# A decoder of two layers on one core: the last layer's start moves into cross attention's last group, and TensorE multiplies for nobody in two waits

## The reference, cut to what matters

```python
x = LN(x + test_time_training(x))                 # a linear model, one SGD step per token
x = LN(x + cross_attention_0(x, ctx, mask))       # one head, width 256, bias 512 x 1601
x = LN(x + mixture_of_experts(x))                 # 8 experts, top 2, hidden 1024
x = LN(x + causal_self_attention(x))              # 16 heads of 16
x = LN(x + cross_attention_1(x, ctx))             # 16 heads of 16, rotary, out @ Wo.T + bo
h = (x - mean) * rsqrt(var) * gamma + beta        # layer norm inside the last block
x = LN(x + 0.5 * (silu(h @ W1 + b1) @ W2 + b2))   # W1, W2 dequantised, hidden 1024
```

## Time and profile before

| | |
|---|---|
| median of 3 runs | 2063.3 us |
| profiled execution | 2063.18 us, its span 2061.1 us |
| TensorE busy | 1811.4 us (88%), mean clock 0.936 |
| VectorE busy | 1428.5 us (69%) |
| ScalarE busy | 1063.8 us (52%) |
| GpSimd busy | 710.5 us (34%) |

### The profile page before, as it was taken

The page is one execution under the profiler, slowest core; times in us unless marked ns, Lnnn a source line. Parts: engine busy times, 40 slices in busy tenths (PEclk is TensorE's granted clock), DMA queues, the critical chain, the costliest instruction groups (busy, mean ns, idle before and its releaser), DMA issues. The chain is left out here.

```text
span 2061.1 us, 32786 instructions
## 1 busy us (share of the span) xinstructions
PE 1811.4 (88%) x12562; PEld 1031.0 (50%) x12562; DVE 1428.5 (69%) x2391; ACT 1063.8 (52%) x1706; POOL 710.5 (34%) x786
## 2 busy tenths in 40 slices
PE   8888888893999999947999989869999999998687
PEld 4677655672888888833333365512222222221455
DVE  1432368774677777767778558889999999991644
ACT  1111144450656555523666723318888888787242
POOL 0574286501344444423233014321541212100543
PEclk9999999995999999977899999959999999998789
DMA  5014087756466666534111037611311101000101
GB/s 183 19 62 135 35 296 249 257 205 251 180 258 263 259 249 239 184 115 131 25 32 34 9 132 212 198 37 58 95 47 24 34 17 34 17 17 1 51 1 41
DMA packets 107743, 241.62 MB, mean 117 GB/s; under 512 B 28362, under 2 KB 79086, under 8 KB 103600
## 3 DMA queue, kind: packets, MB, share of 16 engines
q1 hardware_dynamic: 80484, 199.43, 27.5%
q0 software_dynamic: 24992, 38.00, 6.6%
q10 hardware_dynamic: 2112, 2.10, 0.3%
HBM read 182.09 MB, written 56.79 MB: 116 GB/s over the span
## 5 line engine op out<-in xcount | busy, mean ns | idle before, releaser
L1772 DVE TENSOR_REDUCE Eh_maxima<-Eh_max 128x2 f32<-128x802 f32 x512 | 474.7, 987 | 22.9 <-PE Eh_max L1657 16.0
L1760 ACT ACTIVATE Eh_probs<-Eh_pair 128x1024 f32<-128x1024 f32 (+1 forms) x288 | 287.8, 999 | 117.0 <-PE Eh_pair L1696 117.0
L1152 PE MATMUL C_y<-C_x_high,C_W 128*128 128x256 f16 x1472 | 250.2, 274 | 1.5 <-DVE C_x_low L1389 1.5
L1657 PE MATMUL Eh_max<-Eh_KS,Eh_QS 49*128 49x401 f16 x1024 | 198.4, 358 | 51.9 <-DVE Eh_maxima L1772 41.7
L1719 PE MATMUL Eh_av_ps<-Eh_probs,E_V 128*17 128x512 f32 (+1 forms) x1664 | 226.0, 616 | 0.0
L1152 PE MATMUL C_y<-C_x_low,C_W 128*128 128x256 f16 x736 | 201.5, 274 | 0.0
L1772 DVE TENSOR_REDUCE Dh_maxima<-Dh_max 128x2 f32<-128x1024 f32 x128 | 152.1, 1221 | 46.7 <-PE Dh_max L1665 42.7
L1760 ACT ACTIVATE Eh_probs<-Eh_single 128x512 f32<-128x512 f32 x272 | 161.5, 594 | 21.3 <-PE Eh_single L1696 21.2
L1657 PEld LDWEIGHTS Eh_max<-Eh_KS,Eh_QS 49*128 49x128 f16 x1024 | 50.5, 94 | 240.8 <-DVE Eh_maxima L1772 201.3
L1500 POOL DMA_DIRECT2D Eh_KS<-E_kd x64 | 37.2, 582 | 356.5 <-PE Eh_pair L1696 350.7
L1152 PEld LDWEIGHTS C_y<-C_x_high,C_W 128*128 128x128 f16 x1472 | 144.6, 98 | 18.9 <-issue 1.9
(11 more groups left out here) (367 smaller groups left out, 3702.2 us busy)
## 6 DMA issues: line engine op xcount, KB each, us to landing
C_W<-w_split SPq DMA_DIRECT2D x23, 3072.0 KB, 11.1
w_split<-B_w_parts SPq DMA_DIRECT2D x24, 768.0 KB, 4.6
B_places<-in_w_experts_dram SPq DMA_DIRECT2D x18, 768.0 KB, 6.0
Eh_KS<-E_kd POOLq DMA_DIRECT2D x64, 150.1 KB, 3.3
C_tail<-in_expert_tail_dram SPq DMA_DIRECT2D x23, 384.0 KB, 8.0
A_QT<-in_w_experts_dram SPq DMA_DIRECT2D x8, 768.0 KB, 5.2
w_split<-A_QT SPq DMA_DIRECT2D x8, 768.0 KB, 6.8
early_ctxT<-in_ctxT_dram SPq DMA_DIRECT2D x6, 800.5 KB, 5.8
```

The source lines that it names most:

```text
L1152: last = mm(y_ps[n % Y_BANKS][:, i, :], W[:, u, a, at_w:at_w + P], x[:, s % 2, k, :], start=(q == 0), stop=(q == len(parts) - 1))
L1657: last = self.nc.tensor.matmul(bank[:, a, 0:self.cw], self.QS[r, slot, p, qt * P:(qt + 1) * P], self.KS[r, slot, p, k0:k0 + self.cw], star ...
L1760: self.nc.scalar.activation(dst, src, ACT.Exp, scale=1.0 / SCORE).then_inc(self.exp_done, 1)
L1772: self.nc.vector.tensor_reduce(self.maxima[:, g % 2, :, p * TPB + qt, c], self.max_ps[n % 2][:, :, 0:self.cw], AX_X, ALU.max).then_inc(sel ...
```

## The change

Nothing of what is computed changes. In parts:

1. `spin` is new: n float32 products of the identity with 512 columns, whose result nobody reads. Eight stand in TensorE's list before the first `turn` of the expert layer, thirteen, behind the wait for the weights, before the first `turn` of self attention.
2. In self attention's first stage VectorE normalises batch 0 before it begins to mix batch 1, and SP issues the loads of constants behind all loads of rows.
3. VectorE no longer waits for `all_stored` in `Heads`; to make that safe the small tiles of the maxima are placed with the keys and queries. Both `Heads` blocks leave out GpSimd's drain at the end.
4. A class `LastStart` holds what the last block begins with. Its 15 items (`START_ITEMS`) go into the last group of cross attention, the first behind its third S and then one behind every second S; all are shift, `attended` and `project` of batches 0 to 2, and the two half turns of batch 0's normalised tokens. They use the two banks of the maxima. VectorE does all copies, sums and norms there, GpSimd the bias additions, the inverse deviations and the low part of batch 0. The token of group 14 waits until the banks are free. SP loads Wo, bo, bv, gamma and beta before the first rows of maxima.
5. No barrier for clearing semaphores stands between cross attention and `phase_last`; that phase begins with turning batch 1. Batch 3's attention result is turned after four widenings of batch 0, projected in step 1 of batch 1; the turns of batches 2 and 3 come in step 5 of batches 1 and 2. W1's parts stay in SBUF (the weights' order is swapped, W2 is the one stored and loaded).

```diff
+def spin(nc, bank, ident, x, n):
+    for _ in range(n):
+        nc.tensor.matmul(bank, ident, x, start=True, stop=True)
@@ phase_moe, tensor
+            spin(nc, y_ps[0][:].rearrange("p a s -> p (a s)"), ident[:], XT[:, 0, 0:S], 8)
             turn(0)
@@ phase_self, sync
-                places.load_consts(sp)
                 for b in range(1, B):
...
+                places.load_consts(sp)
@@ phase_self, tensor
+                pe.wait_ge(carried.w_loaded, 32)
+                spin(nc, turn_ps[0][:], ident[:], w[:, 0, 0:S], 13)
                 turn(0)
-                pe.wait_ge(carried.w_loaded, 32)
@@ phase_self, vector
                 norm.statistics(dve, 0, sum_ready)
+                norm.normalize(dve, 0)
                 mix(1, 0)
-                norm.normalize(dve, 0)
                 rest_x(0)
@@ Heads.walk, last step of the walk
+            between = iter(range(len(START_ITEMS)) if self.start is not None and step == GROUPS - 1 else ())
+            scores = 0
             for kind in self.order:
+                if kind == "T":
+                    for i in between:
+                        yield "X", i
...
                 elif kind in "SB":
                     yield "S", s
-                    s += 1
+                    s, scores = s + 1, scores + 1
+                    if scores >= START_AFTER and (scores - START_AFTER) % 2 == 0:
+                        for i in between:
+                            yield "X", i
+                            break
@@ Heads.tensor
+            if kind == "X":
+                if k == 0:
+                    pe.wait_ge(self.read, n)
+                self.start.tensor(pe, START_ITEMS[k])
             if kind == "T":
+                if k == GROUPS - 2 and self.start is not None:
+                    self.start.banks_free(pe)
@@ Heads.vector
-        self.places.all_stored(dve)
...
+            if kind == "X":
+                self.start.vector(dve, START_ITEMS[k])
@@ run_heads
-    with nc.Block() as block:
+    with nc.Block(no_gpsimd_drain=True) as block:
...
+            if heads.start is not None:
+                heads.places.all_stored(sp)
+                heads.start.sync(sp)
@@ new
+START_ITEMS = (("shift",), ("attended", 0, 0), ("attended", 0, 1), ("attended", 1, 0), ("project", 0), ("attended", 1, 1), ("project", 1),
+               ("attended", 2, 0), ("project", 2), ("attended", 2, 1), ("project", 3), ("project", 4), ("project", 5), ("turn", 0), ("turn", 1))
+START_AFTER = 3
+class LastStart:
+    def vector(self, dve, item):
...
+        if kind == "project":
+            j = at[0]
+            after.add_pair(dve, j)
+            if j == 1:
+                after.norm.statistics(dve, 0, after.sum_ready, per=2)
+            if j == 2:
+                self.again(dve, 0)
+            if j == 3:
+                after.norm.statistics(dve, 1, after.sum_ready, per=2)
+            if j == 4:
+                self.normed_again(dve, 0)
+            if j == 5:
+                self.again(dve, 1)
+                after.norm.statistics(dve, 2, after.sum_ready, per=2)
+        if kind == "turn":
+            h = at[0]
+            dve.wait_ge(self.turned, h + 1)
+            v.tensor_scalar(self.HT[:, 0, h, :], after.turn_ps[h], self.gamma[:, h:h + 1], self.beta[:, h:h + 1], ALU.mult, ALU.add).then_inc(self.copied, 1)
+            if h == KD - 1:
+                dve.wait_ge(self.copied, KD)
+                v.tensor_copy(self.HT_parts[:, 0, 0], self.HT[:, 0]).then_inc(self.ht_high, 1)
+                self.normed_again(dve, 1)
+    def pool(self, pool):
...
+        for c in range(B - 1):
+            after.base(pool, c)
+        after.norm.inverse_deviation(pool, 0)
+        norm_in.inverse_deviation(pool, 0)
+        after.norm.inverse_deviation(pool, 1)
+        after.base(pool, B - 1)
+        norm_in.inverse_deviation(pool, 1)
+        after.norm.inverse_deviation(pool, 2)
+        self.low(pool, 0)
@@ phase_last, tensor (all of the old order up to the loop is gone)
             turn(1)
+            for j in range(NF // 2):
+                widen(0, j)
+            pe.wait_ge(copied, 2 * KD)
+            after.attended(pe, B - 1)
             for j in range(NF // 2, NF):
                 widen(0, j)
+            pe.wait_ge(w_loaded, 16)
             for c in range(1, B):
                 for j in range(NF):
                     widen(c, j)
                     narrow(c - 1, j // 2, range(NF // 2) if j % 2 == 0 else range(NF // 2, NF))
+                    if (c, j) == (1, 1):
+                        after.project(pe, B - 1)
+                    if (c, j) == (1, 5):
+                        turn(2)
+                    if (c, j) == (2, 5):
+                        turn(3)
@@ phase_last, scalar
+            act.wait_ge(small_loaded, 32)
             turn(1)
+            for n in range(B * NF):
                 step(n)
+                if n == NF // 2 - 1:
+                    copy_turned(nc, act, XT, turn_ps, B - 1, after.turned, after.copied)
+                if n == NF + 5:
+                    turn(2)
+                if n == 2 * NF + 5:
+                    turn(3)
@@ phase_last, gpsimd
+            norm_out.setup(pool)
+            start.low(pool, 1)
+            low(0)
             norm_in.inverse_deviation(pool, 2)
+            for n in range(1, B * NF):
+                low(n)
+                if n == NF + 1:
+                    after.norm.inverse_deviation(pool, 3)
+                if n == NF + 4:
+                    norm_in.inverse_deviation(pool, 3)
+                if n in (NF + 6, 2 * NF + 6):
+                    start.low(pool, n // NF + 1)
+                if n in (2 * NF + 1, 3 * NF + 1):
+                    norm_out.inverse_deviation(pool, n // NF - 2)
@@ phase_last, vector
+            dve.wait_ge(small_loaded, 32)
             v.tensor_scalar(b2[:], b2[:], 0.5, None, ALU.mult).then_inc(half_b2, 1)
+            step(0)
+            start.again(dve, 2)
+            step(1)
+            step(2)
             dve.wait_ge(half_b2, 1)
+            base(0)
+            for j in range(3, NF):
+                step(j)
             for c in range(1, B):
                 for j in range(NF):
                     step(c * NF + j)
+                    if (c, j) == (1, 0):
+                        start.normed_again(dve, 2)
+                    if (c, j) == (1, 1):
+                        after.add(dve, 3)
+                        after.norm.statistics(dve, 3, after.sum_ready, per=2)
...
+                    if (c, j) == (1, 4):
+                        start.again(dve, 3)
+                    if (c, j) == (2, 0):
+                        start.normed_again(dve, 3)
```

More of the change, by code:

```diff
@@ L1505, with __init__ @@
 class Heads:
-    def __init__(self, ctx, nc, name, n_keys, places, V, ATT, idents, tri, ahead, behind, order):
-        self.nc, self.n_keys, self.causal = nc, n_keys, places.causal
+    def __init__(self, ctx, nc, name, n_keys, places, V, ATT, idents, tri, ahead, behind, order, start=None):
+        self.nc, self.n_keys, self.causal, self.start = nc, n_keys, places.causal, start
         self.places, self.KS, self.QS, self.slots, self.R = places, places.KS, places.QS, places.slots, places.R
@@ L1520, in __init__ @@
         self.L = len(self.tiles)
-        self.chunks = (n_keys + S - 1) // S
+        self.chunks = places.chunks
         self.cw = -(-n_keys // self.chunks)
@@ L1536, in __init__ @@
         self.probs = sb("probs", [P, self.turns * self.ring, S])
[L1537 to L1540, removed]
+        self.maxima, self.top, self.neg_parts, self.neg_rows, self.inv = places.maxima, places.top, places.neg_parts, places.neg_rows, places.inv
         self.av = sb("av", [P, S])
-        self.inv = sb("inv", [P, TPB, STRIPS])
         self.pair_ps, self.single_ps = ps("pair", [P, 2, S]), ps("single", [P, S])
@@ L1836, in __init__, with make_banks @@
             self.need = 48
+    def make_banks(self, ctx):
+        self.turn_ps = [ctx.enter_context(self.nc.psum_tensor(f"{self.name}_turn{i}", [P, S], F32)) for i in range(KD)]
+        self.out_ps = [ctx.enter_context(self.nc.psum_tensor(f"{self.name}_out{i}", [P, 2, D], F32)) for i in range(2)]
     def sync(self, sp):
@@ L1845, in attended, with attended_half @@
     def attended(self, pe, c):
+        for h in range(KD):
+            self.attended_half(pe, c, h)
+    def attended_half(self, pe, c, h):
         if c >= 1:
[L1847 to L1851, removed]
+            pe.wait_ge(self.copied, KD * (c - 1) + h + 1)
+        for t in range(TPB):
+            last = self.nc.tensor.transpose(self.turn_ps[h][:, t * P:(t + 1) * P], self.ATT[:, t, c * D + h * P:c * D + (h + 1) * P], self.ident[:])
+        last.then_inc(self.turned, 1)
     def shift(self, pe):
@@ L1865, in project, with project_pair @@
         for j in range(c * TPB // 2, (c + 1) * TPB // 2):
[L1866 to L1870, removed]
```

(38 more changed lines are left out.)

267 lines of the change are left out of this document (130 added, 137 removed).

## The result

The changed kernel takes 2045.76 us (median of 5 runs, 2039.43 to 2048.59), the kernel before on the same chip 2065.94 (2062.9 to 2068.27): ratio 0.9908, 95% interval 0.9887 to 0.9930, 20.2 us less. Forecast were 28.5 us less, 2034.7, range 2021 to 2047.

| place | forecast | before | after | difference |
|---|---|---|---|---|
| start to the last counting product | 0 | 497.8 | 500.1 | +2.3 |
| from its end to the end of the expert layer | -2.2 | 387.5 | 385.7 | -1.8 |
| self attention's front, to its first maximum | -3.4 | 65.2 | 58.8 | -6.5 |
| self attention's heads | 0 | 235.0 | 234.4 | -0.6 |
| last division to the next phase's first work | -0.1 | 1.5 | 5.4 | +3.9 |

A forecast was written before the change was run, and what follows sets the result against it. Bound: TensorE in the expert layer, TensorE and ScalarE in cross attention's last group, a chain of waits from 1908 to 1975. Terms -2.2 - 1.5 - 3.9 + 7 - 42.6 + 14.7 = -28.5 from 2063.2: 2034.7 us, range 2021 to 2047.

The forecast's parts named there:

- Rival B: Group 15 of cross attention runs at the low clock, costing 12 us, with a slower start after: 2042; chance 0.18.
- C: Rival: the spins do nothing (2037) or run over by 3.6 and 5 us (2045); chance 0.11.
- rival D: Group 15 hides nothing, each item waiting for the one before: 2061 to 2071, slower than before; chance 0.03.
- Part 1: Expert layer's start: eight spins in TensorE's idle hole raise the clock for first turn and products; -2.2 us.
- Parts 2 and 3: Self attention's front, earlier normalisation and spins: -1.5; both attentions, no store wait before first maxima: -3.7, drains 0.2.
- Part 4: Cross attention's group 15 carries fifteen items of the next phase; its last division ends later: +7 us.
- row at 0.50: Profile row, 957 to 992: narrow products kept TensorE busy 29.8 of 35 us, yet the clock stayed at 0.50.
- Part 5: Last division to batch 1's first widening in the last phase: 25 us instead of 67.6, gain 42.6.
- Part 6: Last phase's dense loop: projection and turns +5.7, two stalls for GpSimd's low part +7, low clock +2; +14.7 us.
- A: Rival: no stall in the last phase's dense loop and group 15 at its lower end: 2024; chance 0.2.

The follow-up runs named there:

- e1: Changed kernel without both spin lines (the eight and the thirteen products): 2054.17 us, ratio 0.9944.
- e5: Kernel before, with GpSimd's drain left out at the end of both blocks of heads: 2079.64 us, ratio 1.0093.
- e6: Changed kernel without self attention's thirteen products, the eight kept: 2045.22 us, ratio 0.9920.
- e3: Changed kernel with GpSimd's drain back in self attention's heads and one in cross attention before the next phase is set up: 2040.71 us, ratio 0.9880.
- e2: Changed kernel with GpSimd's drain back at the end of self attention's heads only: 2045.59 us, ratio 0.9916.
- e7: Changed kernel with batch 1's normalised rows made after cross attention's last division, not in group 15: 2045.33 us, ratio 0.9931.
- e9: e8 plus unread TensorE products ahead of both attentions' heads and between the first maxima: 2026.05 us, ratio 0.9803.
- e8: Changed kernel with e3, e4 and e7 combined, plus earlier bias loads and reordered normalisations, additions, turns and narrowing in the last phase: 2019.85 us, ratio 0.9796.
- e4: Changed kernel with turns of batches 2 and 3 and GpSimd's low parts two steps earlier in the last phase: 2044.71 us, ratio 0.9912.

## Why the prediction came out as it did

The time was inside the range, the direction right, the gain 20 us and not 28.5. It lies 1.2 us below the upper end, which had been set for rivals B and C. Neither happened; two other terms were too small by 14 us (drains 8.8, group 15 5.0), and a better front of self attention took 3 of them back. That the time is inside the range is partly luck. (The chances of "same" and "slower", 0.04 together, also don't fit the 0.03 of rival D that they were said to come from.)

- **Part 1** (-2.2): -1.8, with e1 +1.7 without it. Spins ended at 509.3, 1.5 us ahead of the turn.
- **Parts 2 and 3.** The drain apart, the fronts gave more. From phase start to first turn it was 17.9 us, and 17.8 in e5, the other kernel with mixing first; with normalising first it was 14.8, and 14.7 to 16.7 in nine more. The forecast -1.0 took the 0.82 us of the earlier trace rows for the whole wait; in e5 the first batch's rows came early, and the mixing waited 3.21 us for those of the second, with the ready factors behind it. By these fronts the order and the earlier rows together are worth 1 to 3 us; no run parts the two. The stores: 1.9 and 2.1 us (forecast 3.7 in all, measured 4.0). The thirteen products: 0.9 in e6 (forecast 0.5), with the exception of e3.
- **The step that failed** is the sentence "The drain taken from two barriers: 0.2, bounds 0 and 0.8". It measured +8.6. I priced the drain by GpSimd's idle queue at the barrier, as if its work were gone with it. Taken away, it is owed at the next one, and these were the renewal and the program's end, where everybody waits. e2, e3 and e5 show this from both sides. A bound above zero was given for gain, none for loss. e2 took away the 3.9 us of waiting, but by its median no time was won, since the projections behind it took 3.5 us more. What sets the drain's length is open. It is long only where GpSimd has issued transfers since its last one, but no run changed their number, and more of them did not make it longer: 5.45 us behind 219 (92 of them the expert layer's gathers and scatters, which no drain had followed), 9.30 behind 165 in cross attention.
- **Part 4** (+7, bound 12): +12.0, the second term that was too small. I added 16 us of items to 33 of busy time and set the sum against a 44 us window, as if the items would fill its idle time. They take 18 us, and the idle time stays: of 3.5 us of waits for exponentials 1.3 remain, but before the last turn it is 2.6 us and not 0.8, behind VectorE's queue (e7: 2.1). And +12.0 is measured against an execution with 10.3 us of the group at the low level: against the 33.6 us of e5, with none, the items cost 15.8 us, so that only some 2 of their 18 us were hidden. Rival B's price of 12 came by another way: the clock was 0.98. Its row at 0.50 spoke against the rule that activity releases the throttle (the Trainium skill, "TensorE: Matmul & The Clock Gate", What's actually happening); e9, where denser work shortened the low stretches ahead of the same narrow products, speaks for it. Group 15 says nothing on it: it was at the high level in e5 without the items, and partly at the low one in e8 with them.
- **Part 5** (+25 from the last division): 25.05, and 25.0 to 25.8 in e2 to e4, e6 and e7; 23.6 in e1, where 6.8 us of the stretch were at the low level and not 15.5.
- **Part 6** (+14.7): +13.0; the two holes of 3.5 us measured 3.29, each ended by what was named, and e4 took them away.
- **Rivals.** A did not happen. C: the spins did what they should. D: far off; ScalarE's longest waits beside an item were 1.93 us.
- **Nobody's terms.** +2.3 ahead of the change, -2.5 in cross attention's projections and +2.7 in its heads go with where the clock's low stretches fall: up to the last counting product, in code that no kernel here changed, the twelve traces have 497.8 to 506.0 us, and the cross heads to the 14th division took 522.1 to 530.4 us in the ten executions without extra products in them.

## What to carry to other kernels

A drain that is taken out where nobody waits for it is not saved but moved: look at who meets the next one. (A wait that really held an engine is another matter: that for the stores was saved, 4.0 us.) When work is put into the gaps of a group, add it to the engine's busy time and assume that no idle time is filled until the row of each wait says so; take the busy time at the high clock, and see in a second trace how the group varies by itself. A low clock in a stretch costs only if TensorE is waited for there; ask that before bridging it.

## What the runs showed of the hardware

- GpSimd's drain takes 4.0 to 5.5 us as the first one behind the expert layer's gathers and scatters and self attention's loads, and 8.3 to 10.4 behind cross attention's transfers; with no or one or two transfers since the last drain 0.04 to 1.17 us.
- VectorE's four normalisations of 256 columns: 1.38 us alone, 3.19 beside one GpSimd instruction of 2.2, and 3.10 beside two of 1.2.
- In cross attention a group of 32.4 us takes 33.75 when one low stretch of 3.4 us falls in it, and how many groups have one differs from execution to execution; this and the like make the spread of the runs.
